# A graph-network, linear-attention and gated-FFN kernel on one core: row blocks of the gate pass turned by DMA transposes in place of TensorE, with a rebuilt merge of the weights and a rebuilt output pass

## The chip, the cores and the metric

One core of one Trainium2 chip runs the whole program. The metric is the time of one execution in microseconds (us) on the device, the median of several runs.

## The reference

6250 rows of 512 float32 values go through three blocks, each with a residual:

```python
xn = _layernorm(x)
x = x + gnn(xn) + mix(xn)          # gnn: segment_sum(w * xn[src], dst) @ weight + bias, 100000 edges
                                   # mix: linear attention, 8 heads
z = _layernorm(x)
gh = relu(z @ gfc1_w.T + gfc1_b)                     # gate hidden, 6250 x 512
g = (gh @ gfc2_w.T + gfc2_b).mean(axis=1)            # 8 gate values, one set for all rows
W1m = W1 + einsum('be,efd->bfd', g, tv_W1)           # 256 x 512, merged from 8 task matrices
W2m = W2 + einsum('be,edf->bdf', g, tv_W2)           # 512 x 256
h = relu(z @ W1m.T + b1m);  out = h @ W2m.T + b2m
res = z + out
x = x + (res - mean(res)) * rsqrt(var(res) + 1e-5) * lng + lnb
```

The gate values need a mean over all rows, so the rows are passed over twice: once for the gate (the gate pass) and, after the weights are merged, once for the output (the output pass).

## The kernel before

The rows are 49 tiles of 128 rows (the last has 106). `acc[128, 49, 512]` holds them in SBUF throughout. The program is written engine by engine, each engine's list in a fixed order, with semaphores between them. It has these stages in time:

- the head, in which the layernorm, the projection for the graph block and the edge tables are made;
- the edge stage, 196 slots of 512 edges: POOL gathers rows, TensorE sums and places them, VectorE adds them to `acc`; the products of mix and its queries are threaded through the same slots. `row_ticks` isn't used here; the order stands in one loop over slots `s`, ending in slot `NGR - 1`;
- the gate pass. `row_ticks` runs a tick function once for each tile on each engine, the first 8 and the last ones written out and the middle in a hardware loop of 8 ticks. For a tile, ScalarE writes the normalised rows as float32 (`zn`) and as float16 (`zh`), VectorE makes the float16 rest (`zl`), TensorE turns both in eight 128x128 transposes into PSUM (`turn_rows`), VectorE copies the turned tile to `ztg`, and SP stores it to `zt_rows` in DRAM. Four tiles are a quad, and `ztg` holds two quads. For each quad TensorE makes four groups of twelve matmuls (one group in each tick) with the gate weights `G16`, and ScalarE folds each to a row sum through `gjunk`. `free_group` is the wait that keeps a tile from being written to `ztg` before the gate matmuls of the quad two earlier are done;
- the merge: from the eight gate values `gall`, `geye` (the identity times a gate value) and the merges `W1m` and `W2m` with their scales are made, and the eight matrices `tvW2` are loaded. PARTITION_ALL_REDUCE on POOL spreads each largest value over the partitions;
- the output pass. ScalarE recomputes the normalised rows from `acc` (`zq`), TensorE makes the hidden rows of a quad from `xd` (loaded from `zt_rows`) and per tile seven matmuls for the output, VectorE adds (`res`), takes statistics (`bn_stats`), ScalarE scales (`zr`), VectorE multiplies by `lngb`, POOL adds `lnbb` to `acc` and then `acc` to `zr` into `ob`, and SP stores `ob`.

Semaphores that the text names: `gf_done` counts finished gate groups, `turned_kept` the stores of `ztg`, `two_made` the finished statistics of a quad.

## Time and profile before

| | before |
|---|---|
| time, median of 3 runs | 1876.7 us (1876.6 to 1879.99) |
| the profiled execution | 1881.32 us, its span 1879.5 us |
| mean granted TensorE clock | 0.93 |
| PE busy | 1549.2 us (82%) |
| DVE busy | 1212.1 us (64%) |
| POOL busy | 919.1 us (49%) |
| ACT busy | 702.8 us (37%) |

PE is TensorE's matmuls, PEld its weight loads, DVE is VectorE, ACT ScalarE, POOL GpSimd, SP the engine that issues most DMAs. The span runs from the first to the last instruction. Busy shares over the whole span say little here, since each stage has its own limit; the trace has to be read stage by stage.

### The profile page before, as it was taken

Reading aid. Unit: us, or ns where it says so; the run is one execution under the profiler, and the core shown is the slowest. Engines: PE = TensorE matmul, PEld = TensorE weight load, DVE = VectorE, ACT = ScalarE, POOL = GpSimd, SP = SyncE. Lnnn points to the kernel's source line nnn. Section 1 sums busy time; section 2 is a strip of 40 time slices with the busy share of each in tenths; the row PEclk is TensorE's granted clock in tenths of the full one; section 3 lists DMA queues with packets and bytes.
Section 4 is the critical chain, followed back from the end, with each engine's and each line's share of the span. In section 5 each row is a group of like instructions: output and inputs, shape, how many; then the busy total and the mean of one; then the engine's idle time right before and its main releaser. Section 6 shows DMA issues by size and latency. Waiting matters only on the chain.

```text
span 1879.5 us, 27602 instructions
## 1 busy us (share of the span) xinstructions
PE 1549.2 (82%) x8551; PEld 672.3 (36%) x8551; DVE 1212.1 (64%) x2230; ACT 702.8 (37%) x1098; POOL 919.1 (49%) x919
## 2 busy tenths in 40 slices
PE   0699968888988898787888888888887799888883
PEld 0345423333333333243333333333333444453331
DVE  7888734554544555456776777676667666468996
ACT  3266522222222232212332333333333677425554
POOL 3000056666666666646666666666663000016776
PEclk9799989999999999978999999999999799989996
DMA  5389777777777777746666666666665422333332
GB/s 182 127 297 324 272 238 227 220 214 224 225 227 223 227 225 225 213 123 193 194 197 200 196 195 196 195 196 197 196 197 154 159 78 79 115 115 107 134 134 83
DMA packets 149271, 353.64 MB, mean 188 GB/s; under 512 B 24773, under 2 KB 30551, under 8 KB 149155
## 3 DMA queue, kind: packets, MB, share of 16 engines
q0 software_dynamic: 62720, 205.57, 37.0%
q1 hardware_dynamic: 84926, 145.42, 22.6%
q8 instruction: 60, 0.98, 0.2%
q10 hardware_dynamic: 1509, 1.21, 0.2%
q14 instruction: 56, 0.46, 0.1%
HBM read 287.93 MB, written 65.38 MB: 188 GB/s over the span
## 4 chain that ended last, share of the span: by engine, by line
PE 37%; DVE 18%; another core or an unknown queue 16%; issue 14%; ACT 9%; DMA 2%; DVEq 1%; ACTq 0%; SPq 0%; POOL 0%; POOLq 0%
PE bank L1550 26%; PE bank L1659 4%; PE bank L1633 4%; ACT mb L642 2%; PE bank L1649 2%; DVE acc L1164 2%; ACT part L636 2%; DVE st L1058 1%; PE bank L1592 1%; ACT qT L663 1%; DVE res L1511 1%; DVE zr L1539 1%; DVE zl L1092 1%; ACT zh L598 1%
## 5 line engine op out<-in xcount | busy, mean ns | idle before, releaser
L850 POOL DMA_INDIRECT rows<-y_rows,idxT x784 | 767.9, 979 | 613.3 <-issue 395.1
L1164 DVE SCALAR_TENSOR_TENSOR acc<-bank,maskt,acc 128x512 f32 x392 | 275.4, 744 | 200.3 <-remote 107.4
L642 ACT ACTIVATE mb<-bank,ones,ncols 128x512 f32<-128x512 f32 x98 | 76.6, 782 | 527.5 <-remote 290.6
L1550 PE MATMUL bank<-KVP,qT 128*128 128x512 f16 x588 | 168.2, 446 | 72.1 <-ACT qT L663 62.1
L1649 PE MATMUL bank<-rows,hots 128*32 128x512 f16 x2352 | 194.3, 402 | 38.7 <-issue 35.1
L1659 PE MATMUL bank<-part,plc 128*128 128x512 f32 x392 | 212.1, 622 | 12.3 <-ACT part L636 6.0
L636 ACT COPY part<-bank 128x512 f32<-128x512 f32 x196 | 113.0, 577 | 192.7 <-remote 145.5
L1550 PE MATMUL bank<-Wg,xtb 128*128 128x512 f16 x588 | 143.3, 396 | 25.6 <-DVE xtb L1103 25.5
L1550 PE MATMUL bank<-Wk,xta 128*128 128x512 f16 x588 | 142.9, 394 | 1.2 <-issue 1.0
L1633 PE MATMUL bank<-xr,kh 128*128 128x512 f16 x392 | 124.8, 402 | 16.7 <-DVE kl L1191 13.4
L1649 PEld LDWEIGHTS bank<-rows,hots 128*32 128x32 f16 x2352 | 78.1, 143 | 166.4 <-issue 144.3
L1550 PE MATMUL bank<-Wq,xta 128*128 128x512 f16 x588 | 135.4, 380 | 0.0
L1550 PE MATMUL bank<-ztg,G 128*128 128x512 f16 (+1 forms) x624 | 134.8, 368 | 0.0
L1550 PEld LDWEIGHTS bank<-KVP,qT 128*128 128x128 f16 x588 | 61.0, 111 | 174.5 <-ACT qT L663 81.4
L1205 DVE SCALAR_TENSOR_TENSOR kf<-bank,cols,mb 128x512 f32<-128x512 f32 x49 | 36.8, 750 | 111.8 <-ACT mb L645 86.6
L1184 DVE SCALAR_TENSOR_TENSOR kf<-bank,cols,mb 128x512 f32<-128x512 f32 x49 | 36.6, 746 | 106.9 <-issue 55.7
L874 POOL PARTITION_ALL_REDUCE mxa<-mx x1 | 0.3, 350 | 206.5 <-DVE mx L1462 206.5
L1659 PEld LDWEIGHTS bank<-part,plc 128*128 128x128 f32 x392 | 68.2, 193 | 67.3 <-issue 45.1
L891 POOL TENSOR_TENSOR ob<-zr,acc 128x512 f32<-128x512 f32 x49 | 63.0, 1287 | 55.4 <-DVE zr L1539 53.3
L1550 PEld LDWEIGHTS bank<-Wg,xtb 128*128 128x128 f16 x588 | 56.7, 101 | 92.8 <-DVE xtb L1103 19.7
L1550 PEld LDWEIGHTS bank<-Wk,xta 128*128 128x128 f16 x588 | 55.1, 100 | 76.4 <-issue 22.6
L1550 PE MATMUL bank<-xd,W1m 128*128 128x512 f16 (+1 forms) x312 | 72.6, 387 | 9.9 <-DMA xd<-zt_rows 6.2
(278 smaller groups left out, 2324.0 us busy)
## 6 DMA issues: line engine op xcount, KB each, us to landing
xta<-xt_rows SPq DMA_DIRECT2D x98, 256.0 KB
x_rows<-xhl SPq DMA_DIRECT2D x49, 256.0 KB, 2.6
xt_rows<-xtb SPq DMA_DIRECT2D x49, 256.0 KB, 3.0
y_rows<-yb SPq DMA_DIRECT2D x49, 256.0 KB, 2.5
rows<-y_rows,idxT POOLq DMA_INDIRECT x784
xr<-x_rows SPq DMA_DIRECT2D x49, 256.0 KB
zt_rows<-ztg SPq DMA_DIRECT2D x49, 256.0 KB, 2.0
acc<-in_x SPq DMA_DIRECT2D x48, 256.0 KB, 3.1
```

Of the source, the lines that this page charges most:

```text
L598: nc.scalar.activation(to, flat(acc, t), ACT.Identity, scale=rs[:, bass.ds(t, 1)], bias=nb[:, bass.ds(t, 1)]).then_inc(loop.high, 1)
L636: nc.scalar.copy(part32[:, s % 2, :], edge_bank(s)[:, :]).then_inc(part_kept, 1)
L642: nc.scalar.activation(mb[:, :], of[:, :], ACT.Relu, scale=ncols[:, col:col + 1], bias=ones[:, 0:1]).then_inc(f_min, 1)
L850: pool.indirect_dma_start(out=rows[:, slot].rearrange("p a d -> p (a d)"), out_offset=None, in_=y_rows, in_offset=bass.IndirectOffsetOnAxi ...
L891: pool.tensor_tensor(ob[:, b, :], zr[:, b, :], flat(acc, t), ALU.add).then_inc(ob_made, 1)
L1164: nc.vector.scalar_tensor_tensor(out=flat(acc, tile + m), in0=placed_bank(s)[:, :], scalar=maskt[:, m, s:s + 1], in1=flat(acc, tile + m), ...
L1184: nc.vector.scalar_tensor_tensor(out=kf[:, b, :], in0=bank[5][:, :], scalar=cols[:, 1:2], in1=mb[:, :], op0=ALU.mult, op1=ALU.max).then_in ...
L1205: nc.vector.scalar_tensor_tensor(out=kf[:, 0, :], in0=q_bank(t)[:, :], scalar=cols[:, 2:3], in1=mb[:, :], op0=ALU.mult, op1=ALU.max).then_ ...
L1550: ins = nc.tensor.matmul(dest, lhs, rhs, start=(n == 0 and only), stop=(n == len(pairs) - 1), skip_group_check=not only)
L1633: ins = nc.tensor.matmul(bank[c][:, :], (kh, kl)[p][:, b, s], xr[:, b, q, :], start=isinstance(t, int) and t == 0 and i == 0, stop=isinsta ...
L1649: ins = nc.tensor.matmul(edge_bank(s)[W * i:W * i + W, :], hots[:, k, p, :, m + i], rows[:, K4 * (s % RING) + i, q, :], start=n == 0, stop ...
L1659: nc.tensor.matmul(placed_bank(s)[:, :], plc[:, s // WG % 3, s % WG, :], part32[:, s % 2, :], start=True, stop=True).then_inc(placed, 1)
```

## The change

Gate pass: `turn_rows` and the copy to `ztg` are gone. `zh` and `zl` become the two halves of `zhl`, and SP issues one DMA transpose for each tile (`zhl` to `ztg`, 128 partitions by 8 blocks of 128). The normalised float32 rows `zn` are stored as well, to a new DRAM tensor `z_rows`. The store of `ztg` to `zt_rows` comes two ticks after the transpose. POOL adds `lnbb` to `acc` in this pass. The loads of `W1`, `W2`, `tvW1` and two of the matrices `tvW2` are spread over the ticks. The gate weights are turned, and their largest value found, at the end of the edge stage, where in the last slot `place(s - 1)` and `part(s)` change places.

Merge: ScalarE makes `geye`; four of the eight `tvW1` are merged on VectorE and four on TensorE by `geye`; four of the `tvW2` on either. The largest values are spread by a small transpose and a matmul on TensorE (`turn_max`, `spread_max`). POOL splits the bias `b2f` in three.

Output pass: `zq` is loaded from `z_rows`. VectorE sums `res` while it makes it (`accum_out`), ScalarE sums the squared deviations, and VectorE makes `cen` and then `ob` itself, five tiles behind. POOL has no work there.

```diff
-EDGE_BANKS = (4, 6, 7)
+EDGE_BANKS = (6, 7, 4)
+GATE_BANKS = (2, 3, 5, 4)
...
+OUT_LAG = 5
+TV2_PAIRS = ((6, 7), (0, 1), (2, 3), (4, 5))
...
 U = 2 * Q4
+KQ_AT = (T // U - 1) * U
...
+W1_TURNED = (4, 5, 6, 7)
+W2_TURNED, W2_MERGED = TV2_PAIRS[:2], TV2_PAIRS[2:]
...
+            def load_tv2(i):
+                for e in TV2_PAIRS[i]:
+                    sp.dma_start(tvW2[:, e], tv_W2[e].rearrange("(c p) f -> p c f", p=P)).then_inc(tv2_loaded[i], 16)
+
+            def load_weights(at):
+
+                if at == 0:
+                    sp.dma_start(W1raw[:, :, :], W1.rearrange("(c p) d -> p c d", p=P)).then_inc(small_loaded, 16)
+                if at == 1:
+                    sp.dma_start(W2raw[:, :, :], W2.rearrange("(c p) f -> p c f", p=P)).then_inc(small_loaded, 16)
+                if 2 <= at < U:
+                    load_tv1(at - 2)
+                if KQ_AT <= at < KQ_AT + 2:
+                    load_tv1(U - 2 + at - KQ_AT)
+                if at == KQ_AT + 2:
+                    load_tv2(0)
+
             def tail_stores(g, j):
-                g1, j1 = back(g, j, 1)
+                if exists(g, j):
+                    t, b = tile_at(g, j), j % 2
+                    sp.wait_ge(tail.low, t + 1)
+                    waited(sp)
+                    free_group(sp, g, j)
+                    waited(sp)
+                    sp.dma_start_transpose(ztg[:, j // Q4, j % Q4].rearrange("p a c m -> p (a c) m"),
+                                           zhl[:, b].rearrange("p a d -> p (a d)")).then_inc(z_turned[b], 16)
+                    at_least(sp, z_kept[b], 16 * half_at(g, j))
+                    waited(sp)
+                    sp.dma_start(row_tile(z_rows, t), zn[:, b, :]).then_inc(z_kept[b], 16)
+                if isinstance(g, int):
+                    load_weights(tile_at(g, j))
+                g1, j1 = back(g, j, 2)
                 if exists(g1, j1):
                     t, b1 = tile_at(g1, j1), j1 % 2
-                    sp.wait_ge(tail.turned_out, t + 1)
+                    sp.wait_ge(z_turned[b1], 16 * half_at(g1, j1) + 16)
+                    waited(sp)
                     at_least(sp, tail.turned_kept[b1], 16 * half_at(g1, j1))
+                    waited(sp)
                     sp.dma_start(row_tile(zt_rows, t), ztg[:, j1 // Q4, j1 % Q4].rearrange("p a c m -> p (a c m)")
                                  ).then_inc(tail.turned_kept[b1], 16)
...
             sp.wait_ge(gf_done, C * NQ)
-            for e in range(NE):
-                sp.dma_start(tvW2[:, e], tv_W2[e].rearrange("(c p) f -> p c f", p=P)).then_inc(tv2_loaded, 16)
-            sp.wait_ge(gate_out, 2 * NE)
+            for i in range(1, NE // 2):
+                load_tv2(i)
...
+                gn, jn = back(g, j, -2)
+                if exists(gn, jn) and exists(g, j):
+                    sp.wait_ge(res_made, tile_at(g, j) + 1)
+                    waited(sp)
+                    load_z(tile_at(gn, jn), j % 2)
...
+                    waited(act)
+                    at_least(act, z_kept[b], 16 * half_at(g, j))
                 waited(act)
-                for to in (dest[:, b, :], high):
-                    nc.scalar.activation(to, flat(acc, t), ACT.Identity, scale=rs[:, bass.ds(t, 1)],
-                                         bias=nb[:, bass.ds(t, 1)]).then_inc(loop.high, 1)
+                nc.scalar.activation(dest[:, b, :], flat(acc, t), ACT.Identity, scale=rs[:, bass.ds(t, 1)],
+                                     bias=nb[:, bass.ds(t, 1)]).then_inc(loop.high, 1)
+                if loop is tail:
+                    at_least(act, z_turned[b], 16 * half_at(g, j))
+                    waited(act)
+                nc.scalar.activation(high, flat(acc, t), ACT.Identity, scale=rs[:, bass.ds(t, 1)],
+                                     bias=nb[:, bass.ds(t, 1)]).then_inc(loop.high, 1)
...
+            nc.scalar.activation(root[:, :], epsc[:, :], ACT.Sqrt)
+            gate_weights()
             act.wait_ge(edges_done, 1)
             deviations(tail, 0, 0, Q4)
             row_ticks(act, tail_tick, Q4 * NQ + 6)
 
+            act.wait_ge(gate_in, C + 1)
+            for e in W1_TURNED + tuple(e for e in range(NE) if e not in W1_TURNED):
+                nc.scalar.activation(geye[:, e, :], ident[:, :], ACT.Copy, scale=gall[:, e:e + 1]).then_inc(eye_made, 1)
...
+                g1, j1 = back(g, j, 1)
+                if exists(g1, j1):
+                    t, par, i = tile_at(g1, j1), j1 // Q4, j1 % Q4
+                    act.wait_ge(mean_made, t + 1)
+                    at_least(act, squared, t)
+                    waited(act)
+                    nc.scalar.activation(squares[:, :], res[:, j1, :], ACT.Square, bias=negm[:, par, i:i + 1],
+                                         accum_out=dev2[:, par, i:i + 1]).then_inc(squared, 1)
...
+                if s == TURN + 24:
+                    pool.wait_ge(maxes_made, 3)
+                    pool.partition_all_reduce(mxa[:, 0:1], mx[:, 0:1], P, RMAX).then_inc(maxes_all, 1)
...
+            pool.wait_ge(edges_done, 1)
+            pool.wait_ge(ln_out, 2)
+
+            def tail_tick(g, j):
                 if exists(g, j):
                     t = tile_at(g, j)
-                    pool.wait_ge(zq_made, t + 1)
+                    pool.wait_ge(tail.high, 2 * t + 2)
                     waited(pool)
                     pool.tensor_tensor(flat(acc, t), flat(acc, t), lnbb[:, :], ALU.add).then_inc(based, 1)
...
+            row_ticks(pool, tail_tick, T)
+            pool.wait_ge(ln_out, 4)
+            split(nc.gpsimd, None, b2f, b216, None, pool_link).then_inc(bias_split, 1)
...
+            def gate_largest():
+                dve.wait_ge(graw_loaded, 16)
+                nc.vector.tensor_reduce(mx[:, 0:1], graw[:, :, :].rearrange("p c n -> p (c n)"), AX_X, ALU.max,
+                                        apply_absolute_value=True).then_inc(maxes_made, 1)
...
-                if exists(g1, j1):
-                    t, b = tile_at(g1, j1), j1 % 2
-                    dve.wait_ge(tail.turned, t + 1)
-                    free_group(dve, g1, j1)
-                    nc.vector.tensor_copy(ztg[:, j1 // Q4, j1 % Q4], turned16(b)).then_inc(tail.turned_out, 1)
+                    low_parts(tail, g, j, zn, zhl[:, j % 2, 0, :], zhl[:, j % 2, 1, :], 2)
...
+            def merge_w2(n):
+
+                i, e = n // 2, W2_MERGED[n // 2][n % 2]
+                dve.wait_ge(tv2_loaded[TV2_PAIRS.index(W2_MERGED[i])], 32)
+                at_least(dve, w2_merged, n)
+                nc.vector.scalar_tensor_tensor(out=W2raw[:, :, :], in0=tvW2[:, e], scalar=gall[:, e:e + 1],
+                                               in1=W2raw[:, :, :], op0=ALU.mult, op1=ALU.add).then_inc(w2_merged, 1)
...
-            for e in range(NE):
+            for n, e in enumerate(e for e in range(NE) if e not in W1_TURNED):
+                at_least(dve, w1_merged, n)
                 nc.vector.scalar_tensor_tensor(out=W1raw[:, :, :], in0=tvW1[:, e], scalar=gall[:, e:e + 1],
-                                               in1=W1raw[:, :, :], op0=ALU.mult, op1=ALU.add).then_inc(gate_out, 1)
-                dve.wait_ge(gate_out, NE + e + 1)
+                                               in1=W1raw[:, :, :], op0=ALU.mult, op1=ALU.add).then_inc(w1_merged, 1)
...
+            link(nc.vector.tensor_reduce(mx[:, 5:6], b1m[:, :], AX_X, ALU.max, apply_absolute_value=True))
+            merge_w2(0)
...
-                    dve.wait_ge(zq_made, t + 1)
+                    dve.wait_ge(z_in[b], 16 * half_at(g, j) + 16)
+                    waited(dve)
                     dve.wait_ge(o_done, t + 1)
...
                     nc.vector.scalar_tensor_tensor(out=res[:, j, :], in0=bank[4 + b][:, :], scalar=cols[:, 4:5],
-                                                   in1=zq[:, b, :], op0=ALU.mult, op1=ALU.add).then_inc(res_made, 1)
-                    dve.wait_ge(res_made, t + 1)
-                    if not (isinstance(quad, int) and quad == 0):
-                        dve.wait_ge(two_made, quad)
-                    nc.vector.bn_stats(st6[:, j % Q4, :], res[:, j, :]).then_inc(six_made, 1)
-                if j % Q4 == 0 and not (isinstance(quad, int) and quad == 0):
+                                                   in1=zq[:, b, :], op0=ALU.mult, op1=ALU.add,
+                                                   accum_out=rsum[:, j // Q4, j % Q4:j % Q4 + 1]).then_inc(res_made, 1)
...
+                    nc.vector.reciprocal(rsr[:, par, 0:n], sd4[:, 0:n]).then_inc(r_scale, 1)
+                g5, j5 = back(g, j, OUT_LAG)
+                if exists(g5, j5):
+                    t5, b5, par5, i5 = tile_at(g5, j5), j5 % 2, j5 // Q4, j5 % Q4
+                    at_least(dve, ob_made, t5)
+                    nc.vector.scalar_tensor_tensor(out=cen[:, :], in0=res[:, j5, :], scalar=negm[:, par5, i5:i5 + 1],
+                                                   in1=lngb[:, :], op0=ALU.add, op1=ALU.mult).then_inc(gained, 1)
...
+                if exists(g, j):
+                    dve.wait_ge(res_made, t + 1)
+                    nc.vector.tensor_scalar(negm[:, j // Q4, j % Q4:j % Q4 + 1], rsum[:, j // Q4, j % Q4:j % Q4 + 1],
...
+                    nc.vector.scalar_tensor_tensor(out=ob[:, b5, :], in0=cen[:, :], scalar=rsr[:, par5, i5:i5 + 1],
+                                                   in1=flat(acc, t5), op0=ALU.mult, op1=ALU.add).then_inc(ob_made, 1)
...
-                last = isinstance(quad, int) and quad == NQ - 1
-                if exists(g, j) and (j % Q4 == Q4 - 1 or last):
-                    n = 1 if last else Q4
...
-                    nc.vector.tensor_tensor(zr[:, b, :], zr[:, b, :], lngb[:, :], ALU.mult).then_inc(gained, 1)
...
                     m_product(t)
                 if s == TURN:
                     sum_keys()
-                place(s - 1)
+                if s != NGR - 1:
+                    place(s - 1)
+                else:
+                    part(s)
...
+            pe.wait_ge(graw_loaded, 16)
+            pe.wait_ge(mix_added, T)
+            pe.wait_ge(edge_added, 2 * (NGR - 2))
+            for f in range(C):
+                for o in range(C):
+                    ins = nc.tensor.transpose(bank[GATE_BANKS[f]][:, o * P:(o + 1) * P], graw[:, o, f * P:(f + 1) * P],
+                                              ident[:, :])
+            ins.then_inc(graw_turned, 1)
...
-                if exists(g, j):
-                    turn_rows(tail, g, j, zh[:, j % 2], zl[:, j % 2], 0)
...
-                        pe.wait_ge(tail.turned_out, T if last else Q4 * q + Q4)
+                        for b in range(1 if last else 2):
+                            pe.wait_ge(z_turned[b], 8 * (T + 1) if last else 16 * (Q4 // 2) * (q + 1))
...
+            pe.wait_ge(tv1_loaded, 16 * NE)
+            for n, e in enumerate(W1_TURNED):
+                pe.wait_ge(eye_made, n + 1)
+                for f in range(C):
+                    for m in range(FC):
+                        nc.tensor.matmul(bank[f // 2][:, (f % 2) * F + m * P:(f % 2) * F + (m + 1) * P],
+                                         tvW1[:, e, m, f * P:(f + 1) * P], geye[:, e, :],
+                                         start=n == 0 and f % 2 == 0 and m == 0, stop=False, skip_group_check=True)
+            pe.wait_ge(w1_merged, NE - len(W1_TURNED))
+            for f in range(C):
...
+            add_turned(w7, False)
+            spread_max(1, 1)
+            pe.wait_ge(tv2_loaded[1], 32)
+            add_turned(w0, False)
```

The order of instructions on SP in the gate pass, where the names are DRAM and SBUF tensors, was this in two ticks of the loop before (ISA rows are waits and small register work):

```order
L523 ISA
L69 ISA
L525 ISA
L525 DMA zt_rows<-ztg 128x1024
L523 REGISTER_ALU
L525 ISA
L525 DMA zt_rows<-ztg 128x1024
```

and is this in two ticks of the loop of the changed kernel:

```order
L559 REGISTER_ALU
L563 DMA_TRANSPOSE ztg<-zhl 128x8x128
L567 ISA
L567 DMA z_rows<-zn 128x512
L577 ISA
L577 DMA zt_rows<-ztg 128x1024
L559 REGISTER_ALU
L75 ISA
L563 DMA_TRANSPOSE ztg<-zhl 128x8x128
L75 ISA
L567 ISA
L567 DMA z_rows<-zn 128x512
```

SP issued one DMA for each tile and now issues three, the transpose first, in one queue.

On TensorE the gate pass stood like this before, for two ticks of the loop:

```order
L1592 MATMUL bank<-ident_51,zh 128x128 x4
L1592 MATMUL bank<-ident_51,zl 128x128 x4
L1823 ISA
L69 ISA
L1550 MATMUL bank<-ztg,G_161 128x512 x12
L1588 REGISTER_ALU
L1592 MATMUL bank<-ident_51,zh 128x128 x4
L1592 MATMUL bank<-ident_51,zl 128x128 x4
L69 REGISTER_ALU
L1550 MATMUL bank<-ztg,G_161 128x512 x12
```

and stands like this now:

```order
L1651 MATMUL bank<-ztg,G_168 128x512 x12
L1932 ISA
L75 ISA
L1651 MATMUL bank<-ztg,G_168 128x512 x12
L75 REGISTER_ALU
L1651 MATMUL bank<-ztg,G_168 128x512 x12
```

The eight transposes of a tile are gone and only the groups of twelve gate matmuls are left.

On VectorE in the output pass a tile of the loop was this before, with the statistics of a quad at its end (`hT` is the float16 rest of the hidden rows, twice in a quad):

```order
L1511 SCALAR_TENSOR_TENSOR res<-bank,cols,zq 128x512
L1516 BN_STATS st_59<-res 128x6
L1497 ISA
L1498 SCALAR_TENSOR_TENSOR hT<-h_166,sc,hT 128x512
L1539 TENSOR_TENSOR zr<-zr,lngb 128x512
```

and is this now:

```order
L1614 SCALAR_TENSOR_TENSOR res,rsum<-bank,cols,zq 128x512
L1625 SCALAR_TENSOR_TENSOR cen<-res,negm,lngb 128x512
L1629 TENSOR_SCALAR negm<-rsum 128x1
L1637 ISA
L1637 SCALAR_TENSOR_TENSOR ob<-cen,rsr,acc 128x512
L1597 ISA
L1598 SCALAR_TENSOR_TENSOR hT<-h_173,sc,hT 128x512
```

The statistics are gone, and the multiplication of `zr` has become two operations that read two SBUF tensors each.

## Rows read from the trace of the kernel before

**Rows 1.** Stretches of time, busy us of each engine, granted clock, DMA share, GB/s

```profile
1475.50:1634.30 158.80, 151.05 (x975) 76.19 (x972) 89.94 (x203) 106.63 (x196) 0.00 (x0) 0.99 0.20 77
1634.30:1682.00 47.70, 35.08 (x221) 24.93 (x222) 29.27 (x67) 8.34 (x16) 3.21 (x4) 0.82 0.46 155
1682.00:1872.80 190.80, 148.77 (x612) 56.07 (x610) 163.88 (x246) 106.06 (x155) 129.64 (x96) 0.90 0.33 117
```

**Rows 2.** Groups by shape, 1475.5 to 1634.3: busy us, mean ns, idle before

```profile
L1550 PE MATMUL bank<-ztg,G 128*128 128x512 f16 x576 | 132.5, 381 | 0.0
...
L1424 DVE COPY ztg<-bank 128x1024 f16<-128x1024 f16 x45 | 30.8, 685 | 8.2 <-PE bank L1550 8.2
L1092 DVE TENSOR_TENSOR zl<-zn,zh 128x512 f16<-128x512 f32 x43 | 29.7, 691 | 46.2 <-ACT zh L598 45.7
L598 ACT ACTIVATE zn<-acc,nb,rs 128x512 f32 x32 | 25.9, 808 | 1.0 <-issue 0.5
...
L1592 PE MATMUL bank<-ident,zl 128*128 128x128 f16 x175 | 17.1, 221 | 0.0
L1592 PE MATMUL bank<-ident,zh 128*128 128x128 f16 x172 | 16.8, 220 | 7.6 <-DVE zl L1092 7.4
```

**Rows 3.** Timeline, end of the gate pass: start us, us, instruction, idle before

```profile
1621.64 0.78 ACT L724 ACTIVATE gjunk<-bank,gbias,cols 128x512 f16<-128x512 f32 x1 [2.54 <-PE bank L1550]
...
1624.23 0.78 ACT L724 ACTIVATE gjunk<-bank,gbias,cols 128x512 f16<-128x512 f32 x1 [1.72 <-PE bank L1550]
```

**Rows 4.** Line 525, 1500 to 1540: ns of one issue min/median/max, landing

```profile
L525 SPq DMA_DIRECT2D zt_rows<-ztg x12: 332/332/333, 1500.3 to 1536.5; - x12
...
DMA to landing us min/median/max: 2.0/2.0/2.0
```

**Rows 5.** DMA queue, 1500 to 1600 (31 stores): packets, MB, share of 16 engines

```profile
q1 hardware_dynamic: 4320, 7.87, 20.7%
```

**Rows 6.** DMA, 1457 to 1458.7: all packets, then the queue

```profile
DMA packets 1689, 0.07 MB, mean 38 GB/s; under 512 B 1658, under 2 KB 1663, under 8 KB 1689
...
q1 hardware_dynamic: 1689, 0.07, 64.1%
```

**Rows 7.** Groups by shape, 1710 to 1850, output pass

```profile
L1539 DVE TENSOR_TENSOR zr<-zr,lngb 128x512 f32<-128x512 f32 x37 | 50.0, 1350 | 10.0 <-ACT zr L774 9.5
L883 POOL TENSOR_TENSOR acc<-acc,lnbb 128x512 f32 x32 | 47.4, 1482 | 0.0
...
L1511 DVE SCALAR_TENSOR_TENSOR res<-bank,cols,zq 128x512 f32<-128x512 f32 x37 | 27.4, 740 | 0.5 <-PE bank L1550 0.5
L1516 DVE BATCH_NORM_STATS2 st<-res 128x6 f32<-128x512 f32 x37 | 25.7, 694 | 1.6
...
L1498 DVE SCALAR_TENSOR_TENSOR hT<-h,sc,hT 128x512 f16<-128x512 f32 x18 | 14.7, 819 | 0.0
```

**Rows 8.** Timeline, 1770 to 1773, output pass

```profile
1770.55 1.27 POOL L883 TENSOR_TENSOR acc<-acc,lnbb 128x512 f32 x1
...
1770.74 1.09 DVE L1522 SCALAR_TENSOR_TENSOR nbr<-var,rsr 128x4 f32<-128x4 f32 x1
...
1772.80 0.69 DVE L1539 TENSOR_TENSOR zr<-zr,lngb 128x512 f32<-128x512 f32 x1 [0.97 <-ACT zr L774]
```

**Rows 9.** Timeline, the merge

```profile
1639.07 1.66 DVE L1441 TENSOR_SCALAR geye<-ident,gall 128x128 f32<-128x128 f32 x8
1640.64 10.52 DVE L1446 SCALAR_TENSOR_TENSOR W1raw<-tvW,gall,W1raw 128x1024 f32<-128x1024 f32 x8
...
1652.41 1.95 PE L1550 MATMUL bank<-geye,tvW 128*128 128x128 f32 x16
...
1682.05 0.75 DVE L1511 SCALAR_TENSOR_TENSOR res<-bank,cols,zq 128x512 f32<-128x512 f32 x1 [3.90 <-PE bank L1550]
```

**Rows 10.** Timeline, end of the edge stage and start of the gate pass

```profile
1444.86 1.41 DVE L1164 SCALAR_TENSOR_TENSOR acc<-bank,maskt,acc 128x512 f32 x2 [2.83 <-PE bank L1659]
...
1451.78 2.25 DVE L1386 TENSOR_REDUCE mx<-graw 128x1 f32<-128x2048 f32 x1
...
1456.19 0.69 DVE L1092 TENSOR_TENSOR zl<-zn,zh 128x512 f16<-128x512 f32 x1 [1.65 <-ACT zh L598]
```

**Rows 11.** Timeline, the last tiles

```profile
1858.87 0.74 DVE L1511 SCALAR_TENSOR_TENSOR res<-bank,cols,zq 128x512 f32<-128x512 f32 x1
...
1872.54 0.27 SPq L557 DMA_DIRECT2D out<-ob  x1
```

319 lines of the change are left out of this document (171 added, 148 removed).

## The prediction

> **What bounds the kernel now.** The change leaves the head and nearly all of the edge stage alone, so I read only what comes after. The stretches in [rows 1] split it in three. The gate pass lasts 158.8 us, with TensorE busy for 151 of them at a clock of 0.99: it is bound by TensorE. The merge lasts 47.7 us in which no engine is busy for more than 35, so it is a chain. The output pass lasts 190.8 us, VectorE busy for 164, TensorE for 149 (3.0 us a tile), POOL for 130.
>
> In the gate pass a group of twelve matmuls comes every 2.59 us where nothing else stands between, as the two folds by ScalarE show [rows 3]; one group belongs to each tile. The pass takes 158.8/49 = 3.24 us a tile. The difference of 0.65 us is the eight transposes, 0.22 us each in part overlapped, and the waits for `zl` before them [rows 2].
>
> In the output pass the reader is to see the `zr` multiplication: 1350 ns on average [rows 7], and 0.69 us when POOL isn't in an addition [rows 8]. The same rows show a 128x4 operation that took 1.09 us, from 0.19 us after the start of an addition on POOL to its end. VectorE waits for POOL when both want two SBUF inputs. So some 0.65 us of each tile is lost to POOL. The Trainium skill says the same (SBUF — State Buffer, Who interferes with whom: the shared port pair is an exclusive lock); the trace agrees, by these 1.09 us.
>
> **The gate pass after.** Without transposes TensorE needs 2.59 us a tile. Three other limits come in.
>
> *The ring of two.* `zn`/`zhl` have two buffers, and ScalarE may write `zn` of tile t+2 only when the store of `zn` of tile t has landed. That store stands on SP behind the transpose. The loop over two tiles is: transpose holding SP, h; store to landing 2.0 us [rows 4]; `zn` 0.81, `zh` 0.80 (as `zn`), `zl` 0.69 [rows 2]; five hand-overs at about 0.1, 0.5. Together 4.8 + h. What a transpose holds SP for, no row shows. Below stands one plain issue, 0.33 us [rows 4]; above, one such issue for each of its eight blocks, 2.66. This gives 2.6 and 3.7 us a tile. I take the middle, h = 1.5, as an operation that must be cut in more pieces than a store but is one instruction: 6.3/2 = 3.15, and with small losses **3.2 us a tile**.
>
> *The DMA engines.* 31 stores took 20.7% of 100 us [rows 5], 0.67 us each. There are now two such and a transpose of cost E: 1.34 + E. For E the nearest row is the store of the same bytes, 0.67. Rows with small pieces bound it: 1689 packets, nearly all under 512 bytes, took 0.641 x 1.7 = 1.09 us of 16 engines [rows 6], 10.3 ns each on one engine. 256 KB in pieces of 256 bytes (one row of a block) is 1024 pieces, 0.66 us; in pieces of 2 bytes 131072, 84 us. I take 1.3, twice the store, near the lower row: 2.65 us a tile, under the ring.
>
> *VectorE and POOL.* VectorE loses the copy to `ztg` (0.69). POOL's 49 additions move here, at the moment when `zl` is made. While POOL catches up after `lnbb` is known, about six `zl` wait up to 0.9 us each. I count 1 to 3 us in all.
>
> A rule speaks against this step. The skill (VectorE: DVE Perf Modes, The three transpose paths) gives a 128x128 transpose 1309 ns on the DMA path and 390 ns on TensorE, and one on the DMA path eight times is 10.5 us a tile. The same skill (Advanced Engine Details and Errata, X-Bar Transpose) calls such transposes as fast as plain DMAs. No run here shows either so far.
>
> **Start and end of the pass.** The reduction of 2.25 us and the DVE idle of 2.83 us before the last additions stand in the way of the first `zl`, which ends at 1456.9 [rows 10]. The reduction goes into the edge stage, where VectorE has room; the swap of `place` and `part` saves about 1 us. ScalarE now has the four `G16` copies first, so I count 2 us: first transpose at 1455. In the first eight ticks SP also issues eight loads of 512 KB, at two stores' worth each 1.34 us of DMA. The demand is then 2.65 + 1.34 = 4.0 us a tile, 0.6 to 0.8 above the ring: +5 us. Tile 47 is issued at 1455 + 48P + 5, lands 2 us later, and TensorE then has a whole quad left (10.3 us) and the short last one (2.3). End: 1474.6 + 48P = 1628.2 for P = 3.2, against 1634.3: **-6 us**. One tenth in P is 4.8 us.
>
> **The merge.** Off the chain: `geye` on VectorE (1.66, partly), four of the eight `W1raw` merges (5.3 of 10.5) [rows 9], since TensorE does the other four, 32 matmuls at 1.95/16 = 0.12 us beside them; the split of `b2f` (3.5), now on POOL; and the two `W2m` high parts, now on ScalarE (1.5). Added on VectorE: four merges of `W2raw` at 1.3, of which about two stand before the scale of `W1m` and two beside TensorE. Net about 12 - 3: the first `res` comes some **9 us** sooner after the end of the gate. If TensorE sits at 1.2 GHz for its first hidden groups (clock 0.82 here already [rows 1]), some 3 us of this go.
>
> **The output pass.** VectorE per tile: `res` 0.77 with its gap, an accumulator read that no row of VectorE shows (below nothing, above a further pass of 0.69; I take 0.19 as a short operation), `cen` 0.69, `negm` 0.17, `ob` 0.75, half of an `hT` without POOL in the way (0.75/2), small ones and gaps 0.15: 3.1. TensorE needs 3.0 [rows 1]. I take **3.15 us**. Before: from the first `res` at 1682.05 [rows 9] to the last at 1858.87 [rows 11], 176.8/48 = 3.68. So 48 x 0.53 = **-25 us**. The statistics of a quad (`two_made`, square root, reciprocal) stood between ticks before and are now a tile later in the order, hidden by the lag of five. DMA per quad: 1 MB of `xd`, four loads of `zq` and four stores are twelve times 0.67 = 8.0 us of 12.6, no bound; a `zq` is asked for two tiles (6.3 us) ahead. After the last `res` it took 13.7 us to the last store [rows 11]; the five late tiles take about 1.6 us each with their stores in a ring of two, and 2 more: 10, **-4 us**.
>
> **Sum.** 1881.3 (the profiled execution) - 6 - 9 - 25 - 4 = 1837. The median of the runs is 4.6 us below the profiled one: 1832.7, so **1833 us**.
>
> **Rivals.**
> - *The pass becomes bound by TensorE* (h near 0.4, E under 1.2). For it: the transpose is one instruction and the plain store holds SP for 0.33. Then P = 2.65 and 48 x 0.55 = 26 us go: 1807. Chance 0.2.
> - *The transposes are slow, and the kernel is slower than before.* The other terms give 44 us, so this decides when P passes 3.2 + 44/48 = 4.1, that is E above 2.8 (pieces of 60 bytes or fewer at 10.3 ns) or h above 3.4. With pieces of 32 bytes E = 5.3, P = 6.6: 1833 + 163 = 1996. For it: a transposed block must be written in other pieces than it is read in. Against: nothing in the trace. Chance 0.14. Its far end is that each block is a transfer of its own that waits for the one before, 8 x 2.0 = 16 us a tile, 1833 + 614 = 2447; chance 0.03. By the 1309 ns of the skill's table that far end would be 10.5 + 1.3 a tile, about 2246.
> - *The output pass gives little.* VectorE is freed, but TensorE has only two banks for the output and stalls in the ticks with hidden groups, at a clock of 0.90 already: 3.6 us a tile, 1833 + 22 = 1855. For it: TensorE's 3.0 is close beneath VectorE's 3.1. Chance 0.12.
> - *The forecast*: P of 2.9 to 3.8, 1815 to 1865. Chance 0.51.
>
> **Numbers.** The range reaches below to the TensorE-bound case with a few us to spare, 1798, and above past the forecast and the third rival to the start of the slow case, 1885; beyond lie about 0.15. Within 0.2% (3.8 us), which is about what a measurement of this kernel can tell from no change, only a P near 4.1 ends: 0.03. Slower: 0.17. Faster: 0.80.
>
> **What would show it.** Right: in the gate pass TensorE idle before its groups while it waits for a DMA, SP held for over a microsecond by a transpose, a tile every 3.2 us; no POOL work in the output pass, all VectorE operations there at 0.7 to 0.8 us, a `res` every 3.15 us. Wrong: DMA share near 1 throughout the gate pass (E too small); landing times of transposes over 5 us; VectorE waiting for `zq`; TensorE at half clock in the gate pass because its groups have gaps, when a group would take 5 us.

## The result and the profile after

The changed kernel took 1862.9 us (median of nine runs, 1856.9 to 1866.3) where the kernel before took 1876.7 beside it (nine runs): a ratio of 0.991, 95% interval 0.989 to 0.994. It is faster by 14 us; the forecast was 44. In a second comparison (changed_timed, below) it took 1854.2 against 1880.5, ratio 0.987 (0.984 to 0.991).

The profiled execution took 1865.4 us, its span 1863.6. The same stretches as in [rows 1], read from the same view (busy us of PE, PEld, DVE, ACT, POOL with counts, then granted clock, DMA share, GB/s):

```profile
1459.40:1485.00 25.60, 14.32 (x47) 5.62 (x48) 14.76 (x33) 10.98 (x18) 6.38 (x5) 0.63 1.04 293
1485.00:1631.00 146.00, 116.16 (x492) 49.24 (x491) 69.59 (x150) 95.80 (x177) 72.13 (x45) 0.93 0.87 246
...
1644.80:1692.10 47.30, 39.06 (x235) 29.25 (x236) 24.63 (x56) 9.55 (x20) 4.09 (x5) 0.82 0.36 123
1692.10:1856.50 164.40, 142.20 (x612) 54.35 (x610) 123.92 (x282) 74.80 (x157) 0.00 (x0) 0.95 0.64 217
```

In the gate pass TensorE is now idle for a fifth of the time, and the DMA engines are at 0.87 where they were at 0.20. The output pass has no POOL work, 40 us less on VectorE, and is 26 us shorter. The merge is as long as it was.

What the gate pass waits for, 1500 to 1600 (chain of waits: us in total, times, longest):

```profile
ACT zn L666 <- DMA z_rows<-zn: 17.3, 15, 2.2
ACT zn L666 <- DVE nb L1151: 14.4, 8, 1.8
PE bank L1651 <- DMA ztg<-zhl: 13.2, 6, 3.5
```

ScalarE waits for the landing of the `z_rows` store (the ring of two), and once a quad for `nb`. TensorE waits for transposes. Behind a long wait its clock falls: of two quads of gate matmuls in a row (timeline of PE, 1500 to 1560), the one behind 0.67 us of idleness took 10.53 us, the one behind 3.48 us took 12.22, and the granted clock was 0.63 from 1531.7 to 1536.3, against 1.00 before and behind. TensorE still waits for the next transposes afterwards, so this is not what sets the pace.

```profile
1517.67 10.53 PE L1651 MATMUL bank<-ztg,G 128*128 128x512 f16 x48 [0.67 <-DMA ztg<-zhl]
1531.67 12.22 PE L1651 MATMUL bank<-ztg,G 128*128 128x512 f16 x48 [3.48 <-DMA ztg<-zhl]
```

The new operation itself, all 49 of it (ns of SP held, min/median/max), and the queue over the same 100 us, in which 29 transposes, 29 stores of `z_rows` and 30 of `zt_rows` were issued:

```profile
L563 SPq DMA_TRANSPOSE ztg<-zhl x49: 1237/1277/2012, 1459.4 to 1631.2; - x49
L577 SPq DMA_DIRECT2D zt_rows<-ztg x49: 332/332/556, 1468.5 to 1637.7; - x49
```

```profile
DMA packets 39583, 23.40 MB, mean 234 GB/s; under 512 B 31919, under 2 KB 31919, under 8 KB 39581
...
q1 hardware_dynamic: 39581, 23.38, 83.5%
```

One turn of the ring, from the timeline (start us, us, instruction, idle before); the `zn` at the end takes the buffer that the store has freed, 6.55 us after the `zn` at the start had begun to fill it:

```profile
1529.85 0.81 ACT L666 ACTIVATE zn<-acc,nb,rs 128x512 f32 x1 [1.82 <-DVE nb L1151]
...
1531.50 0.69 DVE L1168 TENSOR_TENSOR zhl<-zn,zhl 128x512 f16<-128x512 f32 x1 [2.07 <-ACT zhl L671]
...
1532.46 1.24 SPq L563 DMA_TRANSPOSE ztg<-zhl  x1
...
1534.02 0.33 SPq L567 DMA_DIRECT2D z_rows<-zn  x1
...
1536.40 0.81 ACT L666 ACTIVATE zn<-acc,nb,rs 128x512 f32 x1 [1.84 <-DMA z_rows<-zn]
```

And the small multiplication that makes `nb` late, 1500 to 1600 (ns, min/median/max), then one of the eight with the addition beside it, which ends within 0.03 us of it (timeline, start us, us):

```profile
L1149 DVE TENSOR_SCALAR rs<-rs x8: 1022/1025/1033, 1500.6 to 1596.2; - x8
```

```profile
1527.49 1.62 POOL L962 TENSOR_TENSOR acc<-acc,lnbb 128x512 f32 x1 [1.20 <-ACT zhl L671]
1528.12 1.02 DVE L1149 TENSOR_SCALAR rs<-rs  x1
```

A transpose holds SP for 1.28 us and lands 3.1 us after its issue (median). It moves its 256 KB in 31919/29 = 1100 small packets, and takes by estimate (83.5 - 59 x 0.67)/29 = 1.5 us of all 16 engines, 0.67 being a store by [rows 5].

The merge on TensorE (timeline; it answers to [rows 9]):

```profile
1650.05 10.13 PE L1955 MATMUL bank<-geye,tvW 128*128 128x128 f32 x64 [1.02 <-ACT geye L807]
1660.01 1.95 PE L1961 MATMUL bank<-ident,W1raw 128*128 128x128 f32 x16
...
1679.70 0.38 PE L1974 MATMUL bank<-maxdiag,ones 2*128 2x2 f32 x2
1685.21 5.08 PE L1651 MATMUL bank<-xd,W1m 128*128 128x512 f16 x12 [5.13 <-DVE W2m L1591]
1690.23 0.39 PE L1651 MATMUL bank<-krows,qrows 3*128 3x512 bf16 x1
```

VectorE, beside it, has its four experts done in half the time:

```profile
1649.65 5.25 DVE L1539 SCALAR_TENSOR_TENSOR W1raw<-tvW,gall,W1raw 128x1024 f32<-128x1024 f32 x4 [0.24 <-DVE gT L1517]
```

Four experts of W1 are 32 matmuls in the code and 64 records here: a float32 product of 128x128 is two records of 0.12 us. And the first accumulation of the output, 1690.23, stands behind a hidden group that waited 5.13 us and then ran at half its usual speed, 5.08 us where the group at 1691.85 took 2.75. The granted clock was 0.53 there, and 0.50 from 1646 to 1654, so the first of the four experts ran slowly too.

The output pass, 1710 to 1830: the stretch as a whole, then groups by shape (beside [rows 7]):

```profile
1710.00:1830.00 120.00, 112.42 (x473) 42.66 (x473) 92.03 (x210) 57.85 (x119) 0.00 (x0) 0.99 0.69 231
```

```profile
L1637 DVE SCALAR_TENSOR_TENSOR ob<-cen,rsr,acc 128x512 f32<-128x512 f32 x37 | 27.8, 751 | 11.0 <-DVE cen L1625 6.8 <-DMA out<-ob 3.9
L1614 DVE SCALAR_TENSOR_TENSOR res<-bank,cols,zq 128x512 f32<-128x512 f32 x36 | 26.9, 747 | 16.9 <-PE bank L1651 16.9
L1625 DVE SCALAR_TENSOR_TENSOR cen<-res,negm,lngb 128x512 f32<-128x512 f32 x36 | 26.7, 741 | 0.0
...
L1598 DVE SCALAR_TENSOR_TENSOR hT<-h,sc,hT 128x512 f16<-128x512 f32 x19 | 14.1, 745 | 0.0
```

The 1350 ns operation is gone and `hT` is down from 819 to 745. `res` waits for TensorE now, 16.9 us of 120. TensorE is busy for 112.4 of the 120 us, 3.0 us a tile, and waits for another 6.8 for `xd`; VectorE is busy for 92.0, 2.5 us a tile. VectorE no longer sets the pace.

### The profile page after: what moved, and what is told of

Same layout as the page of the kernel before. It is cut to its first block and busy times, and to the rows that moved or that the text cites. A ratio compares the mean times of both kernels' runs of the same rounds, so it can differ in the third digit from the quotient of the medians.

```text
span 1863.6 us, 27212 instructions
## 1 busy us (share of the span) xinstructions
PE 1547.4 (83%) x8173; PEld 657.4 (35%) x8173; DVE 1150.6 (62%) x2206; ACT 670.8 (36%) x1109; POOL 872.6 (47%) x874
## 3 DMA queue, kind: packets, MB, share of 16 engines
q10 hardware_dynamic: 1509, 1.21, 0.2%
## 5 line engine op out<-in xcount | busy, mean ns | idle before, releaser
L1760 PE MATMUL bank<-part,plc 128*128 128x512 f32 x392 | 217.5, 635 | 18.6 <-issue 9.0
L1651 PE MATMUL bank<-ztg,G 128*128 128x512 f16 (+1 forms) x624 | 139.0, 386 | 32.1 <-DMA ztg<-zhl 18.2
L1651 PE MATMUL bank<-Wk,xta 128*128 128x512 f16 x588 | 147.8, 405 | 0.0
L962 POOL TENSOR_TENSOR acc<-acc,lnbb 128x512 f32 (+1 forms) x49 | 79.7, 1632 | 112.1 <-ACT zhl L671 73.9
L1651 PEld LDWEIGHTS bank<-ztg,G 128*128 128x128 f16 x624 | 60.2, 102 | 111.8 <-issue 47.9
L1760 PEld LDWEIGHTS bank<-part,plc 128*128 128x128 f32 x392 | 68.8, 195 | 73.6 <-issue 47.3
L1168 DVE TENSOR_TENSOR zhl<-zn,zhl 128x512 f16<-128x512 f32 x49 | 34.8, 710 | 86.1 <-ACT zhl L671 86.0
L1651 PEld LDWEIGHTS bank<-Wk,xta 128*128 128x128 f16 x588 | 56.4, 103 | 78.8 <-issue 27.5
```

The source lines that it names most:

```text
L962: pool.tensor_tensor(flat(acc, t), flat(acc, t), lnbb[:, :], ALU.add).then_inc(based, 1)
L1168: nc.vector.tensor_tensor(dest, full[:, j % 2, :], high, ALU.subtract).then_inc(loop.low, 1)
L1651: ins = nc.tensor.matmul(dest, lhs, rhs, start=(n == 0 and only), stop=(n == len(pairs) - 1), skip_group_check=not only)
L1760: nc.tensor.matmul(placed_bank(s)[:, :], plc[:, s // WG % 3, s % WG, :], part32[:, s % 2, :], start=True, stop=True).then_inc(placed, 1)
```

## The stages, in every profile of this study

The kernels under one letter ran on one chip beside the kernel before; for the first pair the chip is not on record. Chips differ: the kernel before took 1867.9 us on A, 1726.0 on B and 1880.5 on C. In its two profiles the whole difference lies ahead of the edge end, 1448.8 against 1296.9. The three stages behind it repeat, so I compare them one by one. "Edge end" is the end of the last addition of an edge group to `acc`, "gate" runs from there to the reduction that makes `gsq`, "merge" on to the first `res`, "output" on to the last store's issue. "Pace" is the distance of `zl` from tile 8 to tile 40, over 32.

| profile | chip | edge end | gate | pace | merge | output |
|---|---|---|---|---|---|---|
| before | - | 1448.8 | 186.5 | 3.32 | 46.7 | 190.5 |
| again_before | B | 1296.9 | 187.4 | 3.32 | 47.5 | 190.3 |
| after | - | 1452.9 | 191.9 | 3.41 | 47.3 | 164.4 |
| again_after | A | 1444.5 | 193.3 | 3.42 | 44.5 | 163.4 |
| changed_timed | C | 1441.7 | 193.7 | 3.41 | 46.6 | 161.0 |
| gate_store_first | A | 1439.4 | 182.2 | 3.06 | 47.6 | 164.4 |
| gate_no_additions | A | 1438.8 | 189.5 | 3.34 | 48.6 | 165.1 |
| gate_by_tensor | A | 1432.4 | 197.3 | 3.48 | 45.8 | 164.5 |
| gate_no_z_store | B | 1290.7 | 173.4 | 2.92 | 47.5 | 165.3 |
| gate_halves | B | 1287.8 | 206.4 | 3.68 | 45.9 | 164.5 |
| end_reordered | B | 1293.7 | 192.9 | 3.41 | 40.5 | 161.2 |
| edge_as_before | C | 1450.4 | 195.4 | 3.41 | 45.4 | 164.1 |
| gate_scales_early | C | 1447.5 | 181.8 | 3.07 | 47.6 | 161.3 |
| reordered_all | C | 1452.9 | 179.7 | 3.09 | 39.2 | 163.2 |

By the means of the rows in which a stage is that of the changed kernel as it is (after, again_after, changed_timed and end_reordered's gate pass), the change costs 6 us in the gate pass, gives 1 in the merge and 27 in the output pass: 22 in all. The runs gave 14, then 26. In the first pair of profiles the stages give 20 and the later edge end takes 4 back, which is the 16 us between the two. Of the kernel before there is no profile on chip C, so for the 26 it is not shown where the rest lies.

## The experiments

**again_after, again_before.** Both kernels unaltered.

> The changed kernel once more, unaltered, for the scatter of one profiled execution. In the first profile the edge stage ended 4.1 us later than in the kernel before (1452.93 against 1448.83). If that is scatter of the row gathers, this profile has the last edge instruction 2 us or more away from 1452.9. If it belongs to the change (gate weights' maximum, the earlier load and the swapped place and part on TensorE), it stays within 1 us of 1452.9. The gate pass should again take 192 us (within 2) and the output pass 164 (within 1).

> The kernel before once more, unaltered. The edge stage, which no experiment so far touches, ended at 1452.9, 1444.5, 1439.4, 1438.8 and 1432.4 us in five profiles of the changed kernel and its variants, against 1448.83 in the one profile of the kernel before. If this is scatter, this profile ends the edge stage anywhere in 1430 to 1455, while the three stages behind it repeat: gate pass 186.5, merge 46.7, output pass with its drain 190.5, each within 1.5 us. If the gate pass differs by 5 us or more, the stages cannot be compared from single profiles.

The edge stage of the changed kernel ended at 1444.5, 8.4 us from its first profile, and that of the kernel before, on chip B, at 1296.9. The other stages came back within 1.5 us, but for the merge of the changed kernel (44.5 against 47.3). So the 4.1 us by which the edge stage was longer in the first pair are no finding.

**gate_by_tensor: what are the DMA transposes worth?** TensorE turns the rows again; the store to `zt_rows` comes one tick behind, and `zn` also waits until TensorE has turned the tile two earlier.

```
 def tail_tick(g, j):                      # TensorE
+    if exists(g, j):
+        turn_rows(tail, g, j, zhl[:, j % 2, 0], zhl[:, j % 2, 1], 0)
 ...
-    sp.dma_start_transpose(ztg[...], zhl[:, b]...).then_inc(z_turned[b], 16)
+    nc.vector.tensor_copy(ztg[:, j1 // Q4, j1 % Q4], turned16(b1)).then_inc(tail.turned_out, 1)
```

> The gate pass turns its rows on TensorE again (8 transposes of 0.22 us a tile into banks 0 and 1, VectorE's copy of 0.69 us to ztg), as in the kernel before; the rest of the changed kernel stays, z_rows store and GpSimd's additions too. By the terms of the kernel before TensorE then needs 8 x 0.22 + 12 x 0.381 / ... = the 3.7 us a tile that the kernel before took (177.2 over 48). If the DMA transposes are worth what is between 3.7 and 3.39 to 3.58 they gave 6 to 15 us: gate pass 195 to 207 us against 191.9, median 1866 to 1878. Rival: the DMA transposes gave nothing or cost (in the kernel before the gate pass from edge end to the last sum took 186.5, less than the changed kernel's 191.9): gate pass 185 to 190 us, median 1855 to 1861.

Gate pass 197.3, against 193.3 in the changed kernel on the same chip: in this order of the queue the DMA transposes give 4 us. (The 3.7 us a tile that was expected of TensorE is more than the kernel before took, 3.32; measured here is 3.48.) The median was 1849.5 (1836 to 1854), ratio 0.989 (0.984 to 0.994), which cannot be told from the changed kernel, and its edge stage ended 12 us earlier. The rest of the change costs this stage 197.3 - 187.0 = 10 us, more than the transposes bring. Which part of the rest costs it here (the `z_rows` store, POOL's additions, the weight loads) no run shows. Nor was TensorE's turning tried with the store ahead, as in the next run, so what the transposes are worth in that order is open.

**gate_store_first: the ring of two.** SP stores `zn` first, then transposes.

```
+    sp.wait_ge(tail.high, 2 * t + 1)
+    at_least(sp, z_kept[b], 16 * half_at(g, j))
+    sp.dma_start(row_tile(z_rows, t), zn[:, b, :]).then_inc(z_kept[b], 16)
     sp.wait_ge(tail.low, t + 1)
     ...
     sp.dma_start_transpose(...).then_inc(z_turned[b], 16)
-    at_least(sp, z_kept[b], 16 * half_at(g, j))
-    sp.dma_start(row_tile(z_rows, t), zn[:, b, :]).then_inc(z_kept[b], 16)
```

> SyncE issues the store of the float32 rows (z_rows) before the DMA transpose of the same tile, waiting for zn alone; all else is as in the changed kernel. Theory 1 (the ring of two zn buffers sets the pace: zn 0.81, zh 0.80, zl 0.69, the transpose's 1.24 on SyncE, issue and landing 2.1, hand-overs, over two tiles = 3.3 to 3.4 a tile): the store leaves the long loop, what is left is the loop of the zhl buffers (zh 0.80, zl 0.69, transpose landing 3.1 to 3.5, hand-overs 0.3, over two tiles = 2.5) and the 16 DMA engines (83.5% of 3.39 = 2.83 a tile), so the gate pass goes at 2.9 to 3.0 a tile and gets 17 to 23 us shorter, median 1842 to 1848. Theory 2 (ScalarE waits for nb, which VectorE makes late since GpSimd's addition holds its small instruction; 14.4 of 100 us): the pace stays within 0.1 of 3.39, median 1858 to 1866. Theory 3 (the DMA engines at 83.5% are as full as they get): also no change.

Pace 3.06, gate pass 182.2 (11 us less), median 1841.7, ratio 0.986 (0.984 to 0.988). Of the three theories only the first foresaw a gain, so the ring set the pace; but the gain is short of its 17 to 23 us, and the pace above its 2.9 to 3.0. Its waits and queue, 1500 to 1600, show the next bound:

```profile
ACT zn L668 <- DVE nb L1153: 11.7, 7, 1.8
...
ACT zhl L673 <- DMA ztg<-zhl: 7.4, 11, 1.9
PE bank L1653 <- DMA ztg<-zhl: 7.3, 4, 2.0
ACT zn L668 <- DMA z_rows<-zn: 6.7, 3, 3.3
```

```profile
q1 hardware_dynamic: 43333, 26.57, 97.0%
```

**gate_no_additions: is it the wait for `nb`?** POOL leaves out the addition of `lnbb`.

```
-    pool.tensor_tensor(flat(acc, t), flat(acc, t), lnbb[:, :], ALU.add).then_inc(based, 1)
+    pool.nop(nofuse=True).then_inc(based, 1)
```

> GpSimd leaves out the 49 additions of lnbb to the rows in the gate pass (so the output lacks that term); all else is as in the changed kernel. Theory 1 (the ring of two zn buffers through the z_rows store sets the pace): the wait for nb goes (the 128x4 multiplication on rs falls from 1026 ns to about 170), but the same time is waited for the store instead; pace 3.3 to 3.39, gain 0 to 4 us. Theory 2 (the wait for nb adds 14.4 us in 100 to the pace, since it comes on top of the loop): gate pass shorter by 14 to 20 us, pace 3.0, median 1843 to 1850. The output pass stays at 3.20 a tile either way.

The multiplication on `rs` fell from 1025 to 170 ns and the wait for `nb` vanished, as both theories had it; the pace went only to 3.34 and the gate pass to 189.5. That is theory 1. In place of `nb` ScalarE waited for the store, now 29 us of 100 (groups by shape, 1490 to 1590):

```profile
L666 ACT ACTIVATE zn<-acc,nb,rs 128x512 f32 x27 | 21.9, 813 | 25.6 <-DMA z_rows<-zn 25.6
...
L666 ACT ACTIVATE zn<-acc,nb,rs 128x512 f32<-128x512 f32 x3 | 2.4, 812 | 3.4 <-DMA z_rows<-zn 3.4
```

So POOL cost this pass about 4 us, and the ring is the bound under it. The median was 1848.2, ratio 0.989 (0.987 to 0.991).

**gate_scales_early: `nb` early, with the store first.** VectorE makes `rs` and `nb` of the next quad ahead of the low part of a quad's fourth tile.

```
 def tail_tick(g, j):                      # VectorE
+    group_work(tail, g, j, scales, 3)
     if exists(g, j):
         low_parts(...)
 ...
-    group_work(tail, g, j, scales, 3)
```

> The z_rows store ahead of the transpose, and VectorE makes rs and nb of the next quad ahead of the low parts of a quad's fourth tile instead of behind them, so that GpSimd's hold on its small multiplication (1026 ns) ends before ScalarE needs nb. The wait for nb was 10.1 of 100 us in the run with the store ahead. If it is part of the pace of 3.08, the pace becomes 2.95 to 3.0, the DMA engines' own time, gate pass 176 to 180 us against 182.2. If the DMA engines alone set it, the wait moves to a DMA landing and the gate pass stays at 181 to 183.

The wait for `nb` is gone, and the pace stayed where it was, 3.07, gate pass 181.8. Waits and queue, 1500 to 1600:

```profile
ACT zhl L673 <- DMA ztg<-zhl: 14.4, 27, 1.7
PE bank L1653 <- DMA ztg<-zhl: 8.6, 5, 2.0
ACT zn L668 <- DMA z_rows<-zn: 4.4, 5, 1.8
```

```profile
q1 hardware_dynamic: 43034, 26.10, 95.9%
```

11.7 us of waiting for `nb` in gate_store_first became 7 more of ScalarE's waiting for transposes. With the ring opened and the 16 DMA engines busy for 96 to 97%, it is they that bound the pass, as far as this shows it.

**gate_no_z_store: the DMA engines.** As gate_store_first, with the store of `z_rows` left out; the output pass loads rows of `x` in its place.

```
-    sp.dma_start(row_tile(z_rows, t), zn[:, b, :]).then_inc(z_kept[b], 16)
+    sp.nop(nofuse=True).then_inc(z_kept[b], 16)
 ...
-    sp.dma_start(zq[:, b, :], row_tile(z_rows, t)).then_inc(z_in[b], 16)
+    sp.dma_start(zq[:, b, :], row_tile(x[0:(T - 1) * P, :], 0 if last else t)).then_inc(z_in[b], 16)
```

> As the run with the store ahead of the transpose, but the store of z_rows is left out and the output pass loads rows of x in its place (so the output is another one, with the same bytes loaded). There the gate pass went at 3.08 us a tile with the 16 DMA engines at 96%. Theory 1 (the DMA engines' time is the bound: two stores at 0.67 and a transpose at about 1.6 are 2.95 a tile): without one store they need 2.28, and the pace falls to what TensorE and ScalarE allow, 2.6 to 2.8 a tile, gate pass 160 to 170 us against 182.2. Theory 2 (ScalarE waiting for nb and the zhl buffers sets 3.08): pace 2.95 to 3.08, gate pass 178 to 182.

Gate pass 173.4, pace 2.92: more than theory 2 allows, less than theory 1 asked. The queue, 1345 to 1415, falls to 70.9% of 70 us, 2.07 us a tile. ScalarE's wait for the store is gone and its wait for transposes is down to 4.0 of 70 us; TensorE's is as before. The longest wait of ScalarE is that for `nb`:

```profile
ACT zn L669 <- DVE nb L1154: 10.7, 6, 1.8
...
PE bank L1654 <- DMA ztg<-zhl: 5.5, 5, 1.5
ACT zhl L674 <- DMA ztg<-zhl: 4.0, 6, 0.7
```

```profile
q1 hardware_dynamic: 28749, 12.50, 70.9%
```

This run takes away the store's bytes and, with them, ScalarE's wait for its landing (6.7 us of 100 in gate_store_first), and does not tell the two apart. Three limits thus lie close: ring 3.4, DMA engines 3.06 and, by these waits alone, `nb` with the `zhl` buffers 2.9. TensorE's 2.59 would be the fourth.

**gate_halves: share the turning.** With the store ahead, the high half by a DMA transpose, the low half by four TensorE transposes.

```
+    sp.dma_start_transpose(ztg[:, j // Q4, j % Q4, 0], zhl[:, b, 0, :]).then_inc(z_turned[b], 16)
 ...
+    for c in range(C):
+        ins = nc.tensor.transpose(turned16(b)[:, 1, c, :], zhl[:, b, 1, c * P:(c + 1) * P], ident16[:, :])
 ...
+    nc.vector.tensor_copy(ztg[:, j1 // Q4, j1 % Q4, 1], turned16(b1)[:, 1]).then_inc(tail.turned_out, 1)
```

> The store goes ahead, and each tile's turning is shared: the high half (128x512 float16) by a DMA transpose issued as soon as zh is there, the low half by four TensorE transposes with VectorE's copy of half the size. If the DMA engines' time is the bound and a transpose of half the size costs them half (0.8 of 1.6), they need 1.34 + 0.8 = 2.15 a tile and the weight loads find room; TensorE then needs between 2.59 (no transposes) and 3.33 (eight, kernel before), about 2.95 to 3.0 a tile: gate pass 170 to 178 us against 182.2 with whole transposes, median 1832 to 1840. Rival 1: half a transpose costs the engines and the queue as much as a whole one (1.6): pace as before, 3.0 to 3.1, gate pass 180 to 184. Rival 2: the hand-overs between two ways of turning hold TensorE up (low half late by VectorE's copy): 3.3 to 3.45, gate pass 190 or more.

Gate pass 206.4, pace 3.68: rival 2, and worse than it said. Half a transpose does cost the engines about half by estimate ((56.2 - 56 x 0.67)/28 = 0.67 us, from 56.2% of 1340 to 1440), but SP is held as long:

```profile
L568 SPq DMA_TRANSPOSE ztg<-zhl x49: 1188/1208/2425, 1293.6 to 1480.5; - x49
```

TensorE was at 81 busy us in 100; the stage has the hand-overs of both ways. Which of them sets 3.68 is open. The median was 1713.1, ratio 0.993 (0.990 to 0.995).

**end_reordered: the merge.**

```
-W1_TURNED = (4, 5, 6, 7)
+W1_TURNED = (5, 6, 7)
 ...
 hidden(0, 0, Q4 * P, [0])
 turn_max(2, 5, 5)
-hidden(0, 0, Q4 * P, [1])
 spread_max(2, 2)
+hidden(0, 0, Q4 * P, [1])
+pe.wait_ge(zd_in[1], 16)
+hidden(1, 1, Q4 * P, [0])
 pe.wait_ge(w2_out, FC)
```

> Only the merge is changed: TensorE turns three of the eight W1 experts instead of four (VectorE merges five), the column of the second maximum goes to TensorE ahead of the second half of the first hidden group, and the first hidden group of the second quad is computed in the 5 us in which TensorE waits for W2m, not behind that wait. Theory (a float32 matmul is two passes of 0.12 us, so that an expert costs TensorE 2.56 us here and not 1.3; and the first res waits behind a 5.08 us hidden group at half clock): W1 done 2.2 us earlier, maximum 1.4 us, hidden group 4 to 5 us: from the last gate sum to the first res 38 to 40 us instead of 47.3 and 44.5, median 1854 to 1858 where the changed kernel has 1862.9. Rival (VectorE's own merges and its chain of small instructions set the length, and ScalarE is busy with hT when the early hidden group needs bank 2): 43 to 46 us, no gain that can be measured.

Merge 40.5, 6 us less than the changed kernel's mean of 46.1; output pass within its scatter. Median 1697.4, ratio 0.981 (0.977 to 0.985); the changed kernel itself was not timed on this chip, so the gain rests on the stage. The run does not price its three edits one by one, but its timeline shows each: three experts in 48 records, the second maximum's column back ahead of a hidden group, and the hidden group of the second quad at 2.75 us instead of 5.08, with the first accumulation right behind:

```profile
1491.76 8.34 PE L1955 MATMUL bank<-geye,tvW 128*128 128x128 f32 x48 [1.02 <-ACT geye L807]
...
1517.74 0.38 PE L1974 MATMUL bank<-maxdiag,ones 2*128 2x2 f32 x2 [0.62 <-DVE maxdiag L1532]
1518.05 2.76 PE L1651 MATMUL bank<-xd,W1m 128*128 128x512 f16 x12
1522.38 2.75 PE L1651 MATMUL bank<-xd,W1m 128*128 128x512 f16 x12 [1.57 <-ACT hT L823]
1525.14 0.38 PE L1651 MATMUL bank<-krows,qrows 3*128 3x512 bf16 x1
```

**changed_timed, edge_as_before: the edge stage.** In edge_as_before the load, the turning, the largest value and the scale of the gate weights are back in their old places too.

> The changed kernel unaltered, timed beside the other three on one chip. The stages behind the edges gained 22 us against the kernel before (gate pass 192.6 against 187.0, merge 45.9 against 47.1, output pass with drain 163.9 against 190.4, means of two profiles each). If the edge stage is neither helped nor hurt, this chip shows 20 to 24 us less than before; if the first comparison's 13.8 holds everywhere, the edge stage costs 8 us more in the changed kernel.

```
-EDGE_BANKS = (6, 7, 4)
+EDGE_BANKS = (4, 6, 7)
 ...
-                if s == TURN + 18:
-                    gate_largest()
 ...
             statistics(tail, 0, 0, Q4)
+            gate_largest()
             scales(tail, 0, 0, Q4)
```

> The changed kernel with its edge stage and the preparation of the gate weights as in the kernel before: the banks, the order of part and place, the load of the gate weights after the last tile's loads, their maximum, transposes and scale after the edges. If the change's 7 to 8 us in the edge stage are real, the edge stage ends 5 to 8 us earlier than in the changed kernel on this chip, and the gate pass takes 3 to 6 us longer for its later weights: the time within 4 us of the changed kernel. If the edge stage is untouched by the change and only scatters, this kernel is 3 to 6 us slower than the changed one.

The changed kernel took 26.4 us less than the kernel before, its edge stage ending at 1441.7; with the edge stage as before the median was 1864.6 against 1854.2, but the six runs of the changed kernel alone span 1845.8 to 1866.9. The two profiles are 12.3 us apart: the edge stage ended 8.7 later, 1.7 are in the gate pass and 3.1 in the output pass, and the merge was 1.2 shorter. That the change makes the edge stage longer has no support; an edge end that moves by 11 us between profiles of the changed kernel leaves open whether it makes it shorter.

**reordered_all.** Store first, `nb` early, no `tv_W2` load in the gate pass, and the reordered merge. Beyond the diffs above:

```
-                if at == KQ_AT + 2:
-                    load_tv2(0)
 ...
-            for i in range(1, NE // 2):
+            for i in (2, 0, 1, 3):
                 load_tv2(i)
```

> Everything together: z_rows store ahead of the transpose, rs and nb early, no tv_W2 load in the gate pass (the pair goes behind it, the pair that VectorE merges first being loaded first), and the reordered merge. Expected against the changed kernel: gate pass 192.6 to 174 to 179 (2 to 4 us of it the 1 MB less in a DMA-bound stage), merge 45.9 to 39 to 42 and 2.5 us in the output pass as in the run end_reordered, so 22 to 28 us less than the changed kernel and 42 to 52 less than the kernel before. Rival: the later tv_W2 loads make VectorE's or TensorE's W2 merge wait, and the merge loses 3 to 6 us of that.

Gate pass 179.7, merge 39.2. Median 1838.7, ratio 0.979 (0.976 to 0.982), 15 us less than the changed kernel on the same chip and 42 less than the kernel before: faster than both. The last eight `zl` of the pass took 27.5 us against 30.4 with the 1 MB in it. Of the 22 to 28 us expected against the changed kernel the runs show 15; the stages show 14.0 in the gate pass and 7.4 in the merge, with 2.2 lost in the output pass, within its scatter (161.0 to 164.4), and an edge stage that ended 11 us later. The rival did not come: the later `tv_W2` loads made no merge wait.

## Why the prediction was off

The sign was right, and the output pass gave nearly what was forecast. The size was wrong: 44 forecast, 14 to 26 measured, 22 by the stages. Two terms failed, the gate pass (11 to 13 us) and the merge (8 us). By its terms:

- **Output pass, -29 (25 + 4).** Measured -26 in the first profile, -27 by the means. Right in size and in what frees VectorE: without POOL every 512-column operation there takes 0.74 to 0.75 us, and a `res` came every 153.7/48 = 3.20 us where 3.15 was forecast. What bounds the pass after was wrong. The forecast has VectorE at 3.1 us a tile, just above TensorE's 3.0; VectorE is busy for 2.5, and the pace is that of TensorE, 3.0 busy and its waits. That the two limits lie so close is luck. The accumulator read, taken as 0.19, is 0.08.
- **Gate pass, -6.** Measured +5 to +7. The mechanism, the ring of two through the store behind the transpose, was right and is shown by gate_store_first. The term mis-sized is its length, 6.3 us for two tiles: from `zn` to the `zn` two tiles on it is 6.8 on average (tiles 8 to 40), and 6.55 in the timeline above. h was taken as 1.5 and is 1.28, but there 0.59 us more stand between the end of `zl` and the store's issue, the next `zn` starts 2.38 us after that issue, and once a quad `nb` was late. P was 3.41 instead of 3.2, 7 us over tiles 8 to 40. The last eight tiles, forecast at P like the rest, took 31 us, 5 more: two loads of `tvW1` and the pair of `tvW2` fall there, and the sum counted only the loads of the first eight ticks. Those took 32 to 33 us where the sum had 31.
- **The DMA engines, E = 1.3.** Measured 1.5, a lucky guess; it did not bind yet. The 1024 pieces of 256 bytes weighed in the prediction were near the truth, 1100 packets, but by estimate each took 1.5 x 16/1100 = 22 ns of an engine and not 10.3. The Trainium skill (Advanced Engine Details and Errata, X-Bar Transpose) expects such transposes to be as fast as regular DMAs. The trace disagrees: 1.5 us against 0.67 for a store of the same bytes. The other rule weighed in the prediction, eight times 1309 ns, does not hold here either: a whole tile's eight blocks landed in 3.1 us.
- **POOL's collisions, 1 to 3 us.** They struck elsewhere than forecast. Six `zl` were to wait while POOL caught up; one did, 1.61 us at 1480.06, 0.2 us after an addition had begun. The others stayed at 692 ns. What waited was the 128x4 multiplication on `rs`, 1025 ns instead of 170, and through it ScalarE. Worth 4 us by gate_no_additions.
- **Merge, -9.** Measured -1. This step failed outright. It read "x16, 1.95 us" as sixteen matmuls, but the code issues eight: each expert on TensorE costs 2 us and more, so that four of them (10.1 us, with a start at half clock) took longer than VectorE's four (5.3). The Trainium skill (FP8 and Floating Point Precision, TensorE Precision Notes) counts four passes through the array for a true float32 product; the trace shows two records and 0.24 us for it, and no run here tells the passes in them apart. And what was said to cost perhaps 3 us, TensorE at half clock in its first hidden groups, struck the third of them and cost 2.3, on top of a wait of 5 us behind which the group had been put. end_reordered gave 6 of the missing 8 us back.
- **The rival of slow transposes** was wrong by a wide margin. The rival of a TensorE-bound gate pass failed because two other limits, the ring and the DMA engines, lay ahead of TensorE. Of the signs of being wrong, TensorE at half clock in the gate pass came in part, behind idle stretches of 3 us and more. The third rival, an output pass bound by TensorE, was right on the engine and wrong on the pace, 3.6 against 3.2.

## What to carry to other kernels

When work leaves a busy engine, work out the next limits of that stage one by one: the longest loop of a buffer ring with everything that stands on its queue, the busy time of the DMA engines with every load that falls there, the small operations that another engine's work can hold up. Here three of them lay within 15% of the old pace, and only an order that opened the first showed the second. A store that frees a buffer belongs ahead of a slow issue on the same queue. Before a row's duration is divided by its count, the count is to be checked against the loop in the code.

## What was not expected of the hardware

- A DMA transpose of 128x1024 float16 held SP for 1.28 us and one of 128x512 for 1.21 (medians): the hold hardly shrank with the size, while the engines' time fell from 1.5 to 0.67 us and the landing from 3.1 to 2.4.
- An operation of 4 columns with an SBUF tensor and no second one took 1025 ns beside POOL's addition, while the 512-column subtraction `zl` beside the same additions took its usual 692. The trace of the changed kernel shows which began first. The multiplication began 0.6 us after the addition and ended with it. For 43 of the 49 additions `zl` had begun just before, and then it was the addition that grew, to 1.68 us on average against 1.26 with no `zl` beside it; the `zl` at 1480.06, behind the start of an addition, took 1.61.
- The same program took 1726 us on one chip and 1868 to 1881 on two others. In the five profiles of the two unaltered kernels, the four whose edge stage ended at 1440 us or later had POOL waiting before 48 to 53 of its 784 gathers, 90 to 106 us in all, for something that the profile calls remote; the one with 1297 us had no such wait. What it is, no run tells. First the changed kernel in its first profile, then the kernel before in again_before (idle of POOL before its gathers, us and times):

```profile
  issue: 394.3, 684
  PE bank L1750: 117.1, 47
  remote: 103.4, 53
```

```profile
  issue: 421.8, 774
  PE bank L1649: 17.6, 10
```
